# Attention over 4096 rows on one core: casts ahead of the exponential that needs a new bias, a rewritten last stretch, and a fifteenth row buffer

## The reference

```
h = relu(layernorm(x))                      # x: 4096 x 256
q, k, v = h @ Wq.T + bq, h @ Wk.T + bk, h @ Wv.T + bv
a = q @ k.T / sqrt(256) + adj + adj         # adj: 4096 x 4096, fp32
out = x + softmax(a, axis=-1) @ v
```

## Time and profile before

| | us |
|---|---|
| median of 3 runs | 775.21 |
| the profiled execution: its time | 770.59 |
| the profiled execution: its span | 768.8 |
| PE busy in the span | 707.3 (92%) |
| DVE / ACT / POOL busy | 586.0 / 449.0 / 415.1 |
| mean granted TensorE clock | 0.986 |

### The profile page before, as it was taken

How to read it: one execution, slowest core, us unless ns; L and a number is a source line. 1 busy time by engine, 2 the same in 40 slices (tenths; PEclk the granted TensorE clock), 3 DMA queues, 4 the chain that set the end, 5 groups by cost and what they waited for, 6 DMA issues and landing times.

```text
span 768.8 us, 14680 instructions
## 1 busy us (share of the span) xinstructions
PE 707.3 (92%) x4799; PEld 476.3 (62%) x4799; DVE 586.0 (76%) x1274; ACT 449.0 (58%) x755; POOL 415.1 (54%) x421
## 2 busy tenths in 40 slices
PE   6779996999999999999999999999999999999777
PEld 5455553666666666666666666666666666666556
DVE  4969975778878878787888878878778687878440
ACT  4879354574657465656657465656474656556543
POOL 1655303565656555665646455655555565635455
PEclk9989998999999999999999999999999999999999
DMA  8469478897989788989889798989898989886452
GB/s 292 117 207 245 146 189 226 199 230 223 236 210 247 207 223 212 243 214 231 234 216 246 201 220 244 226 221 232 208 239 201 240 214 244 216 207 171 114 128 61
DMA packets 93212, 161.06 MB, mean 209 GB/s; under 512 B 20944, under 2 KB 41808, under 8 KB 93136
## 3 DMA queue, kind: packets, MB, share of 16 engines
q1 hardware_dynamic: 68560, 126.54, 62.4%
q10 hardware_dynamic: 24576, 33.59, 17.7%
HBM read 80.35 MB, written 8.39 MB: 115 GB/s over the span
## 4 chain that ended last, share of the span: by engine, by line
DMA 30%; issue 12%; SPq 12%; ACTq 11%; POOL 10%; PE 8%; ACT 5%; DVE 3%; POOLq 0%; DVEq 0%
DMA rows<-in_adj 11%; ACTq L704 10%; SPq L378 10%; DMA out_y<-xy 8%; DMA xT<-rows 6%; POOL wT L564 6%; PE bank L1265 5%; DMA g_pair<-g_scratch 5%; PE bank L1326 3%; ACT wT L722 3%; ACT rows L693 1%; SPq L332 1%; DVE rows L989 1%; POOL a_op L553 1%; DVE rows L962 1%
## 5 line engine op out<-in xcount | busy, mean ns | idle before, releaser
L1265 PE MATMUL bank<-v_sb,wT 128*128 128x256 f16 x3072 | 379.0, 275 | 36.4 <-POOL wT L564 35.5
L564 POOL TENSOR_TENSOR wT<-xT,wT 128x512 f16<-128x512 f32 x256 | 294.9, 1165 | 206.7 <-ACT wT L722 201.9
L1265 PEld LDWEIGHTS bank<-v_sb,wT 128*128 128x128 f16 x3072 | 298.8, 98 | 133.7 <-POOL wT L564 37.8
L1326 PE MATMUL bank<-top,a_op 128*128 128x512 f16 x1344 | 332.7, 381 | 5.9 <-DVE rows L955 1.9
L693 ACT ACTIVATE rows<-rows,exp_bias,exp_scale 128x1024 f32<-128x1024 f32 x128 | 158.7, 1240 | 128.7 <-DVE exp_bias L1020 76.3
L722 ACT CAST wT<-xT 128x512 f16<-128x512 f32 x256 | 153.4, 612 | 102.5 <-issue 39.3
L1326 PEld LDWEIGHTS bank<-top,a_op 128*128 128x128 f16 x1344 | 130.8, 98 | 116.9 <-DVE rows L955 2.9
L989 DVE STREAM_TRANSPOSE rows<-rows 128x1024 f32<-128x1024 f32 x128 | 158.8, 1241 | 51.4 <-ACT rows L693 51.2
L962 DVE CUSTOM_DVE_ANT_0 rows<-bank,rows 128x512 f32<-128x512 f32 x256 | 173.4, 680 | 12.4 <-PE bank L1326 3.3
L947 DVE SCALAR_TENSOR_TENSOR rows<-rows,adj_scale,bank 128x512 f32<-128x512 f32 x64 | 47.8, 746 | 50.5 <-PE bank L1326 50.5
L684 ACT ACTIVATE rows<-rows,adj_scale 128x512 f32<-128x512 f32 x64 | 46.1, 721 | 41.3 <-DMA rows<-in_adj 37.7
(11 more groups left out here) (108 smaller groups left out, 374.9 us busy)
## 6 DMA issues: line engine op xcount, KB each, us to landing
rows<-in_adj SPq DMA_DIRECT2D x128, 512.0 KB, 5.8
xT<-rows SPq DMA_DIRECT2D x512, 64.0 KB, 3.3
xT<-rows ACTq DMA_DIRECT2D x512, 64.0 KB, 3.7
rows<-in_x SPq DMA_DIRECT2D x8, 512.0 KB, 4.9
xy<-in_x SPq DMA_DIRECT2D x32, 128.0 KB, 4.4
g_scratch<-xT SPq DMA_DIRECT2D x16, 256.0 KB, 3.1
out_y<-xy SPq DMA_DIRECT2D x32, 128.0 KB, 4.9
g_pair<-g_scratch SPq DMA_DIRECT2D x15, 256.0 KB, 5.9
```

The costliest lines, as they stand in the source:

```text
L564: nc.gpsimd.tensor_tensor(split_piece(m, 1), exchanged(m), split_piece(m, 0), ALU.subtract).then_inc(split_lo, 1)
L1265: return nc.tensor.matmul(out_ap, stationary, moving, start=first, stop=last)
L1326: last = nc.tensor.matmul(ps[:], s, mv, start=first and k == 0, stop=k == 2, skip_group_check=True)
```

## The change

- `ROW_UNITS` is 15. The space comes from `vn_even` (a buffer of the setup), which now lies in row buffer 14; the first load into that buffer waits until the setup is done with it. `refill` waits for the exchanged rows only where a row is left to load.
- Three semaphores in place of two for each half of the exchanges (`moved_a`, `moved_b`).
- In ACT's period at n % 4 = 0 the first two pairs of exchange DMAs and two casts stand ahead of the first exponential; in the other periods the casts and their DMA pairs stand ahead of `scale_adj`.
- From the second piece of unit 58 on (`LATE` = 233, 23 pieces) the cast is DVE's (`late_high`) and goes to its own place in `top`, which the last scores have left free, so it waits for no weighing. Units 61, 62 and 63 arrive in row buffers 9 to 14 (`late_xT`) and not in `xT`, with semaphores of their own.
- ACT's last stretch is written out: three casts, then the eight exponentials of units 60 to 63 each as soon as possible, with the exchange DMAs between and behind them. DVE's last stretch is written out too.
- The last two output tiles are stored in two halves, one by SP and one by ACT.

```diff
-ROW_UNITS = 14
+ROW_UNITS = 15
+LATE = 4 * (PERIODS - WEIGH_LAG) + 5
+LAST_UNITS = 3
...
+        vn_even = rows[:, 14, :].bitcast(FP16).rearrange("p (u t s d) -> p u t s d", u=2, t=2, s=2)
...
         def arrivals(u):
-            return xT[:, (u + 1) % XT]
+            k = u - PERIODS + LAST_UNITS
+            return late_xT[k] if k >= 0 else xT[:, (u + 1) % XT]
...
             def refill(u, part):
-                sp.wait_ge((moved_b if part else moved_a)[u % 2], 128 * (u // 2 + 1))
                 p, half, t = unit_parts(u)
                 r = 2 * (QUADS * p + 2 * half + part) + t + ROW_UNITS
                 if r < 2 * PERIODS:
+                    sp.wait_ge((moved_b if part else moved_a)[u % XT], 128 * (u // XT + 1))
                     load_rows(r)
...
+            sp.wait_ge(v_moved[0], 64 * (GROUPS // 2))
+            load_rows(14)
             refill(0, 0)
...
             def period(n):                      # ACT
                 p, u = n // QUADS, n - EXP_LAG
-                exponential(u, 0)
-                exchange_b(u - 1, 0, 0)
-                if n < PERIODS:
-                    scale_adj(n)
-                exchange_b(u - 1, 0, 2)
-                high(4 * (n - WEIGH_LAG) + 2)
-                exchange_b(u - 1, 1, 0)
-                high(4 * (n - WEIGH_LAG) + 3)
+                m = 4 * (n - WEIGH_LAG)
+                if n % QUADS == 0:
+                    exchange_b(u - 1, 0, 0)
+                    high(m + 2)
+                    exchange_b(u - 1, 0, 2)
+                    high(m + 3)
+                    exponential(u, 0)
+                    exchange_b(u - 1, 1, 0)
+                else:
+                    exponential(u, 0)
+                    exchange_b(u - 1, 0, 0)
+                    high(m + 2)
+                    exchange_b(u - 1, 0, 2)
+                    high(m + 3)
+                    exchange_b(u - 1, 1, 0)
+                scale_adj(n)
                 exchange_b(u - 1, 1, 2)
                 exponential(u, 1)
...
+            def late_high(m):                   # DVE
+                u = m // 4
+                if u < PERIODS - LAST_UNITS:
+                    dve.wait_ge(moved_a[u % XT], 128 * (u // XT + 1))
+                    dve.wait_ge(moved_b[u % XT], 128 * (u // XT + 1))
+                else:
+                    dve.wait_ge(moved_last[u - PERIODS + LAST_UNITS], 256)
+                nc.vector.tensor_copy(split_piece(m, 0), exchanged(m)).then_inc(split_hi_late, 1)
```

More of the change, by code:

```diff
@@ L224, in attention_kernel @@
         split_hi = sem("split_hi")
+        split_hi_late = sem("split_hi_late")
         split_lo = sem("split_lo")
@@ L315, in arrival_free, with landing @@
                     eng.wait_ge(g_stored[b], 32 * (GROUPS // 2))
-            wait(eng, split_lo, 4 * (u - XT + 1))
+            k = u - PERIODS + LAST_UNITS
+            if k < 0:
+                wait(eng, split_lo, 4 * (u - XT + 1))
+            if k == 0:
+                for v in (PERIODS - 8, PERIODS - 7):
+                    eng.wait_ge(moved_b[v % XT], 128 * (v // XT + 1))
+            if k > 0:
+                for v in (PERIODS - 6, PERIODS - 5):
+                    eng.wait_ge((moved_b if k == 2 else moved_a)[v % XT], 128 * (v // XT + 1))
+        def landing(u, part):
+            k = u - PERIODS + LAST_UNITS
+            return moved_last[k] if k >= 0 else (moved_b if part else moved_a)[u % XT]
         block = ctx.enter_context(nc.Block())
@@ L471, in _ @@
             for slot in range(XY):
-                sp.wait_ge(stored[slot], 16 * len(range(slot, TILES, XY)))
+                halves = (TILES - 2) % XY == slot or (TILES - 1) % XY == slot
+                sp.wait_ge(stored[slot], 16 * (len(range(slot, TILES, XY)) + halves))
         @block.gpsimd
@@ L886, in period, with store_rest @@
                     high_query(p + 1)
-                high(4 * (n - WEIGH_LAG) + 5)
-            for n in range(SETUP, PERIODS + WEIGH_LAG):
-                period(n)
+                high(m + 5)
+            def store_rest(t):
+                act.wait_ge(y_done, t + 1)
+                act.dma_start(out[t * P + P // 2:(t + 1) * P, :], xy[P // 2:P, t % XY, :]
+                              ).then_inc(stored[t % XY], 16)
+            for n in range(SETUP, PERIODS):
+                period(n)
+            u = PERIODS - EXP_LAG
+            exchange_b(u - 1, 0, 0)
+            high(LATE - 3)
+            exchange_b(u - 1, 0, 2)
+            high(LATE - 2)
+            high(LATE - 1)
+            exponential(u, 0)
+            exchange_b(u - 1, 1, 0)
+            exponential(u, 1)
+            exchange_b(u - 1, 1, 2)
+            exponential(u + 1, 0)
+            exchange_b(u, 0, 0)
+            exponential(u + 1, 1)
+            exchange_b(u, 0, 2)
+            exponential(u + 2, 0)
+            exchange_b(u, 1, 0)
+            exponential(u + 2, 1)
+            exchange_b(u, 1, 2)
+            exponential(u + 3, 0)
+            exchange_b(u + 1, 0, 0)
+            exponential(u + 3, 1)
+            exchange_b(u + 1, 0, 2)
+            exchange_b(u + 1, 1, 0)
+            exchange_b(u + 1, 1, 2)
+            for v in (u + 2, u + 3):
+                for k in range(2):
+                    exchange_b(v, k, 0)
+                    exchange_b(v, k, 2)
+            store_rest(TILES - 2)
+            store_rest(TILES - 1)
         @block.vector
@@ L1257, in period @@
                     finish(2 * p - 3)
-            for n in range(SETUP, PERIODS + WEIGH_LAG + 1):
+            for n in range(SETUP, PERIODS):
                 period(n)
+            u = PERIODS - EXP_LAG
+            finish_12(PERIODS - 1)
+            bias(TILES - 2)
+            bias(TILES - 1)
+            late_high(LATE)
+            late_high(LATE + 1)
+            turn(u, 0)
+            turn(u, 1)
+            late_high(LATE + 2)
+            sums(TILES - 4)
+            turn(u + 1, 0)
+            turn(u + 1, 1)
+            late_high(LATE + 3)
+            finish(TILES - 4)
+            late_high(LATE + 4)
+            late_high(LATE + 5)
+            late_high(LATE + 6)
+            sums(TILES - 3)
+            turn(u + 2, 0)
+            turn(u + 2, 1)
+            for m in range(LATE + 7, LATE + 11):
+                late_high(m)
+            turn(u + 3, 0)
+            turn(u + 3, 1)
+            finish(TILES - 3)
+            for m in range(LATE + 11, LATE + 15):
+                late_high(m)
+            sums(TILES - 2)
+            for m in range(LATE + 15, LATE + 19):
+                late_high(m)
+            sums(TILES - 1)
+            for m in range(LATE + 19, 4 * PERIODS):
+                late_high(m)
+            finish(TILES - 2)
+            finish(TILES - 1)
         @block.tensor
```

39 lines of the change are left out of this document (25 added, 14 removed).

## The result

The changed kernel takes 747.49 us (median of 4 runs, 744.88 to 753.32) where the kernel before takes 776.73 beside it: a ratio of 0.9632, interval 0.9566 to 0.9698. Repeated later beside other runs of before it took 751.6 (six runs, 746.04 to 757.84; ratio 0.9709, 0.9663 to 0.9754). The forecast was 750.3, range 742 to 760. The profiled executions are 770.59 and 744.88, 25.7 apart; the prediction's sum was 24.9.

A forecast was written before the change was run, and what follows sets the result against it. The middle was taken as bound by PE, with only its holes to be won. 11.4 us there plus 13.5 in the last stretch make 24.9, and 775.2 less this gave 750.3 us, range 742 to 760.

The forecast's parts named there:

- The pair's start: Third piece at n % 4 = 0: casts ahead of the exponential remove 0.98 us in all 14 pairs, 14 us.
- What is late next: Third piece at n % 4 = 1: POOL's wait for `g_pair` replaces the removed hole, 12 us lost (4 before).
- `g_pair` doesn't bind: Rival for n % 4 = 1: the load lands earlier, no waits there, the middle wins 18, 743.7 us; chance 0.2.
- The third place: First piece at n % 4 = 3: 1.5 of 7 us left if PE stands at the earlier third piece, else 7.
- The middle in sum: Between the ends: loss falls from 25 to 13.5 us, 11.4 us won, with bounds 0.5 and 25.
- The fifteenth buffer: ACT's 37.7 us of waits for rows go, but 0 us is gained beyond the other terms.
- The last stretch: The last 28 pieces: PE ends at 752.7 in place of 766.1, 13.5 us won.
- rival 3: The last stretch gains nothing, since units still come one by one: 763.8 us; chance 0.05.
- the holes: Last stretch: PE held up 1.1 us at unit 59's second piece, 1.4 at unit 60, 0.4 for hand-overs.
- The cast: DVE's 128x512 cast in the last stretch taken as 0.62 us, between 0.28 and 0.69; DVE busy 27 us in 37.
- rival 1: Port lock in the last stretch: casts and low halves exclude each other, 1.44 to 1.85 us a piece, 754.7 us; chance 0.25.

The follow-up runs named there:

- e1: The kernel before with ACT's new period order alone (14 row buffers, last stretch as before): 757.85 us, ratio 0.9782 to before.
- e3: The kernel before with ACT's new order and 15 row buffers, last stretch as before: 759.41 us, ratio 0.9800 to before.
- e4: The full change without ACT's new order in the scoring periods (15 buffers, new last stretch): 760.45 us, ratio 0.9805 to before.
- e9: The kernel before with the load of `g_pair` issued a period earlier, ahead of the x rows: 773.04 us, ratio 0.9972 to before.
- e6: The full change with the load of `g_pair` issued a period earlier, ahead of the x rows: 738.55 us, ratio 0.9540 to before.
- e8: The full change with both the earlier `g_pair` load and another order of DVE's last stretch: 737.99 us, ratio 0.9544 to before.
- e5: The full change run again, unaltered: 751.60 us, ratio 0.9709 to before.
- e10: The full change with DVE's 23 late casts made by a tensor_tensor naming a PSUM buffer as second operand: 751.34 us, ratio 0.9707 to before.
- e7: The full change with DVE's last stretch reordered, unit 59's casts ahead of the sums and unit 61's transposes: 750.41 us, ratio 0.9700 to before.

## Why the prediction was right, step by step

**The pair's start: right.** 14 us were to go and 14.2 went, in the change and wherever ACT's order was put in (e1, e3), and nowhere else (e4, e9).

**What is late next: right in kind, somewhat high in size.** The wait for `g_pair` took the hole's place: 12 us forecast, 13.0, 10.8, 10.2, 8.1, 7.3 and 6.4 in six profiles with the new order, 9.3 on average. e6 and e8 show that it is this load and nothing behind it. The average start of the sums of +4.7 that the prediction used hides the scatter: only pairs with a late load pay (in the change's profile three of the fourteen cost 1.4 to 1.7 us each and seven nothing). The rival "`g_pair` doesn't bind" (743.7) falls, but the change's own 6.4 lies half way between its 0 and the forecast's 12.

**The third place: the size about right, the reason not borne out.** 1.5 us were to be left at n % 4 = 3; 2.5 and 2.7 are. The prediction's reason was that PE stands 1 us at n % 4 = 1, and that without this stand the 7 us stay. In e6, where PE no longer stands there, 4.7 us are lost, but in e8, with the same middle, only 2.5, as in the change. e9 keeps 7.9 with the order of before. The smaller loss goes with ACT's new order (1.7 to 4.7 us in the eight profiles with it, 4.0 to 7.9 in the three without), whether PE stands at n % 4 = 1 or not; by which step is open.

**The middle in sum.** 11.4 us forecast (its own terms, 25 less 13.5, give 11.5). The losses over periods 8 to 63 were 25.7 in all before; they are 9.7 in the change's profile, 15.6 in e5's and 12.2 in e10's: 16.0, 10.1 and 13.5 won. The first of these profiles has its first piece at 131.42 us where before has 128.02; e5 has it at 128.03 with the same kernel, so these 3.4 us are scatter of the setup. Together with the last stretch: 16.0 + 11.9 - 3.4 = 24.5 of the 25.7 between the profiled executions; the rest lies between the first piece and period 8 (12.40 us, now 11.25) and behind PE's end.

**The fifteenth buffer: 0, right as far as can be measured** on top of the order (e3 to e1). With the order of before it was worth 4.5 us.

**The last stretch: 13.5 forecast, 11.9 measured**, so rival 3, that it gains nothing, falls. The mis-sized term is the holes: 1.1 + 1.4 + 0.4 = 2.9 forecast, 4.3 measured. The larger stands at unit 59's *first* piece and not at its second: its cast at 709.43 is behind the sums, whose third operation takes 0.95 us, and unit 61's two transposes, 2.38. The prediction had counted the transposes only for unit 60, and had 3 us for all sums and finishes. The hole of 1.1 that the prediction hung on `finish` of tile 28, waiting for unit 58, is 0.32: this `finish` did not wait, and behind it the cast took 1.20 us beside POOL. The 1.4 at unit 60, behind sums and two transposes, came as forecast; 0.67 at unit 61 was not in the sum.

**The cast: its duration wrong, with little consequence, and that by a narrow margin.** 0.62 us was taken, nearest to a 128x512 subtraction; it is 0.38 alone and 1.38 in alternation with POOL. The prediction had DVE busy 27 us of 37; it is busy 36.9 of 41.2, waits inside its operations included. The lock's price was the step of rival 1: 1.44 to 1.85 us a piece. It is 1.30, just below PE's 1.31, so from unit 61's second piece on PE has no hole; e10 took the lock away and won nothing on balance. The Trainium skill, "SBUF — State Buffer", Who interferes with whom, has an instruction hold the shared pair for its whole length, and the other block fully. The traces agree that each holds the other up; by that sentence a piece would take 1.157 + 0.38 = 1.54 us, an estimate from the lengths alone, and the traces show 1.30. Which part of an operation excludes the other is not shown.

The middle was thus won by 1.3 us less to 4.6 more than forecast, and the last stretch by 1.6 less. That 750.3 lies between 747.49 and 751.6 owes something to their cancelling; the order of the causes, and the waits that took their place, are what the runs bear out.

## What to carry to other kernels

When a hole at one place of a loop is filled, look for the wait that it was hiding and price that first: here 14 us went, and the loss at the next place rose at once from 4 us to between 6 and 13. Moving one load a period ahead, worth 2 us before, was then worth 7 to 13. Take the distribution of such a wait, not its average, since only the late ones reach the bound, and the latest also cost clock. Two engines that hold each other up need only be, together, below the bound's step; replace the fast form by a slower one without the lock to see its price.

## What the runs showed of the hardware that was not expected

- DVE's cast of 128x512 from fp32 to fp16 takes 0.38 us alone, faster than ACT's 0.62 and than the same cast through a PSUM operand, 0.64 to 0.69. In steady alternation with POOL's subtraction of the same shape it takes 1.38 and the subtraction 1.34 in place of 1.15, 1.30 from start to start, which is less than the two lengths added (1.54).
- DVE's 128x1 operations with two SBUF inputs wait beside POOL: 0.94 and 1.08 us for two that make the last bias, 0.95 for the sums' third, whose shortest takes 0.16. Each of the three ended within 0.02 us of a low half's end.
- Behind six holes of 2.3 to 3.1 us in the middle, TensorE's granted clock was at 1.2 GHz for 3.4 us (e1, e4, e5, e7, e10); behind the holes of 1.65 us and less in the change's first profile it stayed at 2.4 GHz.
